# The out-projection of an attention kernel, made of three f16 products instead of one f32 product

## What is computed

```python
xn = layer_norm(layernorm(x), g1, b1); cn = layer_norm(context, g2, b2)
q, k, v = xn @ Wq.T, cn @ Wk.T, cn @ Wv.T              # 16 heads of 32
attn = softmax(q k^T / sqrt(32), masked)
x = x + (attn v) @ Wo.T + bo                           # the out-projection
x = x + quantised(layernorm(x)) @ quantised(W).T + bias  # blocks of 32, fp6 grid
```

## Time and profile before

| | |
|---|---|
| runs | 4388.42, 4397.13, 4397.69 us; median 4397.13 |
| span of the profiled execution | 4390.0 us (the page gives no other time of it) |
| busy: PE, DVE, POOL, ACT | 97%, 78%, 67%, 65% |
| f32 out-projection, 512 records | 228.7 us |
| mean granted TensorE clock | 0.998 |

### The profile page before, as it was taken

One profiled execution on the slowest core, in us unless ns is written; L12 is line 12 of the kernel. 1 busy time (PEld: TensorE's weight loads), 2 busy tenths in 40 slices (PEclk: granted clock), 3 DMA queues, 4 the chain that ended last, 5 costly groups with the idle time before them and its releaser, 6 DMA issues.

```text
span 4390.0 us, 89201 instructions
## 1 busy us (share of the span) xinstructions
PE 4263.7 (97%) x36496; PEld 1482.1 (34%) x36496; DVE 3402.3 (78%) x3967; ACT 2850.7 (65%) x5184; POOL 2936.2 (67%) x1830
## 2 busy tenths in 40 slices
PE   4999999999999999999999999999999999999999
PEld 2322343223432234322342223422234222342223
DVE  5789667886688865889658896689866898668985
ACT  3388844887448864588655886458854688546884
POOL 2199652996539964499534995359953699426993
PEclk9999999999999999999999999999999999999999
DMA  5266742657326573356733566335664366543664
GB/s 182 70 122 128 155 149 61 126 118 191 120 61 128 118 206 103 69 118 125 192 103 77 117 126 185 107 80 120 128 175 109 80 123 130 165 113 77 126 127 110
DMA packets 193708, 539.67 MB, mean 123 GB/s; under 512 B 28737, under 2 KB 102785, under 8 KB 152082
## 3 DMA queue, kind: packets, MB, share of 16 engines
q0 software_dynamic: 43776, 318.79, 36.3%
q1 hardware_dynamic: 149522, 215.17, 15.8%
HBM read 118.32 MB, written 21.01 MB: 32 GB/s over the span
## 4 chain that ended last, share of the span: by engine, by line
PE 70%; POOL 11%; DVE 7%; DMA 5%; issue 3%; ACT 2%; SPq 0%; POOLq 0%; DVEq 0%; ACTq 0%
PE banks L1116 18%; PE banks L1128 16%; PE banks L1024 16%; PE banks L1084 12%; DVE max_parts L664 5%; PE banks L1159 3%; POOL wkT_wvT_wqT L453 3%; DMA sums<-wkT_wvT_wqT 3%; PE banks L1018 3%; PE banks L993 2%; DMA wdT<-wkT_wvT_wqT 2%; POOL values L545 1%; ACT region L894 1%; POOL region L558 1%; POOL region L531 1%
## 5 line engine op out<-in xcount | busy, mean ns | idle before, releaser
L664 DVE TENSOR_REDUCE max_parts<-banks 128x2 f32<-128x1024 f32 x2048 | 2404.5, 1220 | 362.3 <-PE banks L1084 337.4
L894 ACT ACTIVATE region<-banks 128x512 f32<-128x512 f32 x4096 | 2190.0, 609 | 424.9 <-PE banks L1116 364.4
L453 POOL TENSOR_TENSOR wkT_wvT_wqT<-region 128x1024 f32<-128x1024 f32 x528 | 1348.7, 2752 | 447.0 <-PE banks L1128 327.5
L1116 PE MATMUL banks<-queries_stacked,keys_stacked 98*32 98x512 f16 x16384 | 1267.3, 382 | 12.7 <-ACT values L878 6.2
L1128 PE MATMUL banks<-region,values 128*32 128x512 f32 x8192 | 1075.6, 598 | 18.5 <-ACT region L894 14.8
L1116 PEld LDWEIGHTS banks<-queries_stacked,keys_stacked 98*32 98x32 f16 x16384 | 399.8, 95 | 1001.7 <-ACT region L894 625.5
L1084 PE MATMUL banks<-keys_stacked,queries_stacked 33*128 33x512 f16 x4096 | 716.9, 385 | 6.9 <-DVE max_parts L664 3.5
L1024 PE MATMUL banks<-region,wkT_wvT_wqT 128*128 128x512 f16 x2304 | 558.1, 381 | 12.8 <-DMA wkT_wvT_wqT<-weights_split 10.4
L1084 PEld LDWEIGHTS banks<-keys_stacked,queries_stacked 33*128 33x128 f16 x4096 | 183.4, 93 | 616.5 <-issue 376.5
L453 POOL TENSOR_TENSOR sums<-region 128x1024 f32<-128x1024 f32 x144 | 385.7, 2821 | 0.1
L433 POOL TENSOR_TENSOR region<-row_sums_inverse,region 128x512 f16<-128x512 f32 x80 | 93.3, 1166 | 430.4 <-ACT region L857 429.9
(11 more groups left out here) (99 smaller groups left out, 3247.8 us busy)
## 6 DMA issues: line engine op xcount, KB each, us to landing
wdT<-wkT_wvT_wqT POOLq DMA_DIRECT2D x96, 1024.0 KB, 12.2
wkT_wvT_wqT<-wkT_wvT_wqT POOLq DMA_DIRECT2D x80, 1024.0 KB, 7.6
sums<-wkT_wvT_wqT POOLq DMA_DIRECT2D x72, 1024.0 KB, 7.6
wkT_wvT_wqT<-sums POOLq DMA_DIRECT2D x40, 1024.0 KB, 7.5
region<-in_x SPq DMA_DIRECT2D x24, 1024.0 KB, 8.3
wkT_wvT_wqT<-weights_split SPq DMA_DIRECT2D x8, 3072.0 KB, 20.3
keys_stacked<-region SPq DMA_DIRECT2D x384, 64.0 KB, 2.0
keys_stacked<-sums SPq DMA_DIRECT2D x384, 64.0 KB, 2.0
```

The source lines that it names most:

```text
L453: e.tensor_tensor(SUMS[dst][:, half], PR[i][:, half], PR[i + 1][:, half], ALU.add).then_inc(s_pr, 1)
L664: e.tensor_reduce(mpart[:, buf, :, a, t, c], MXB[parity], AX.X, ALU.max).then_inc(s_mxd, 1)
L894: e.activation(PR[u % 4][:, j * HALF:j * HALF + HALF], score_bank(m % NU, kt, j)[0], ACT.Exp, scale=SCALE).then_inc(s_ex, 1)
L1116: mm = e.matmul(dst[HD * t:HD * t + HD, :], KA[0:STR, ds(ka + (j * C + (u + 1) * P + HD * t), HD)], QA[0:STR, ds(qa[j], HALF)], start=True ...
```

## The change

The out-projection goes through `contract_split`, with f16 high and low parts of both operands, twelve f16 matmuls a tile in place of four f32 ones. `WO` is loaded once at the start, scaled by 64 and split by ScalarE (high) and VectorE (low) into a free part of `QA`, stored to `wo_dram`, and loaded from there in each batch's last unit. The parts of a unit's outputs go into the second half of its `AO` space. For units 0 to 6 GpSimd makes them in the last unit, after its DMA issues: `parts(u)` is a copy to f16 and a subtraction. For unit 7 ScalarE makes the high and VectorE the low part. `x1_tile` scales by 1/64 as it adds.

```diff
@@
     split_dram = nc.dram_tensor("weights_split", [P, 3 * CC * D], F32, kind="Internal").ap()
     wd_dram = nc.dram_tensor("ffn_weights_quantised", [P, CC * D], F32, kind="Internal").ap()
+    wo_dram = nc.dram_tensor("out_weights_split", [P, CC * D], F32, kind="Internal").ap()
     levels = nc.dram_tensor("levels", [2, HALF], F16, kind="Internal").ap()
@@
         AO = QA[:, :].bitcast(F32)
         AO_UNIT = J * HALF // 2
+        ao_part = lambda n, part: QA[:, ds(n * 2 * AO_UNIT + AO_UNIT + part * HALF, HALF)]
+        WOS = WO[:, :, :].rearrange("p c d -> p (c d)")
+        WOP = split(WOS)
+        WO_FIRST = split(AO[:, 2 * AO_UNIT:4 * AO_UNIT])
         X1 = R[:, 0:4096].rearrange("p (i d) -> p i d", i=TT)
@@
             e.dma_start(affine[:, :, :], affine_in).then_inc(s_w, 16)
             tokens(1, x_chunks(0)[:, 1])
+            e.dma_start(WO[:, :, :], woT.rearrange("(c p) n -> p c n", p=P)).then_inc(s_wof, 16)
             e.wait_ge(s_wl, 3)
@@
             context_chunks = lambda b: ctx_in[ds(b, 1)].rearrange("a (c n p) d -> p (a c) n d", p=P, n=4)
+            e.wait_ge(s_wol, 1)
+            e.dma_start(wo_dram, AO[:, 2 * AO_UNIT:4 * AO_UNIT]).then_inc(s_wos, 16)
             e.wait_ge(s_wd, 16)
@@
                                 .broadcast_to([1, H // 2, C])).then_inc(s_mk, 16)
+                if b == 0:
+                    e.wait_ge(s_wos, 16)
                 for par in range(2):
@@
                         if 2 * g + q == NU - 1:
                             e.wait_ge(s_pv, (b * NU + NU - 2) * KT + 4 + 5)
-                            e.dma_start(WO[:, :, :], woT.rearrange("(c p) n -> p c n", p=P)).then_inc(s_wo, 16)
+                            e.dma_start(WOS, wo_dram).then_inc(s_wo, 16)
                         e.wait_ge(s_mc, b * NU + 2 * g + q + 1)
@@
+                        def parts(u):
+                            e.wait_ge(s_an, b * NU + u + 2)
+                            done = b * (NU - 1) + u
+                            ao = AO[:, ds(u * AO_UNIT, HALF)]
+                            e.tensor_copy(ao_part(u, 0), ao).then_inc(s_ah, 1)
+                            e.wait_ge(s_ah, done + 1)
+                            e.tensor_tensor(ao_part(u, 1), ao, ao_part(u, 0), ALU.subtract).then_inc(s_al, 1)
                         if end:
                             merge_last()
+                            parts(0)
                             merge(0, 1, one)
+                            parts(1)
+                            parts(2)
                             merge(1, 2, two)
+                            parts(3)
+                            parts(4)
                             merge(2, 3, three)
+                            parts(5)
+                            parts(6)
                             continue
@@
             for n in range(4):
                 fp6(XB[0][:, n, :]).then_inc(s_xd, 1)
+            e.wait_ge(s_wof, 16)
+            e.wait_ge(s_woh, 1)
+            e.scalar_tensor_tensor(WO_FIRST[:, 1, :, :].rearrange("p c d -> p (c d)"), WOS, W_SCALE,
+                                   WO_FIRST[:, 0, :, :].rearrange("p c d -> p (c d)"),
+                                   ALU.mult, ALU.subtract).then_inc(s_wol, 1)
@@
                         invert_rest()
                         normalise(m, n)
+                        e.wait_ge(s_an, m + 2)
+                        e.wait_ge(s_lh, b + 1)
+                        e.tensor_tensor(ao_part(n, 1), AO[:, ds(n * AO_UNIT, HALF)], ao_part(n, 0),
+                                        ALU.subtract).then_inc(s_ll, 1)
@@
                     e.wait_ge(s_op, b * TT + i + 1)
                     e.wait_ge(s_xb, b * TT + i + 1)
-                    e.tensor_tensor(X1[:, i, :], out_bank(i), X1[:, i, :], ALU.add).then_inc(s_x1, 1)
+                    e.scalar_tensor_tensor(X1[:, i, :], out_bank(i), 1.0 / W_SCALE, X1[:, i, :],
+                                           ALU.mult, ALU.add).then_inc(s_x1, 1)
                     e.wait_ge(s_x1, b * TT + i + 1)
@@
                 e.activation(WD[:, :, n * P:n * P + P], PS[:, n % 2, :].rearrange("p (c t) -> p c t", c=CC),
                              ACT.Copy).then_inc(s_tc, 1)
+            e.wait_ge(s_wof, 16)
+            e.wait_ge(s_cst, 2)
+            e.activation(WO_FIRST[:, 0, :, :].rearrange("p c d -> p (c d)"), WOS, ACT.Copy,
+                         scale=W_SCALE).then_inc(s_woh, 1)
             e.wait_ge(s_mdr, 32)
@@
                         outputs()
                         row_sums(m, KT)
+                        e.wait_ge(s_an, m + 2)
+                        e.activation(ao_part(n, 0), AO[:, ds(n * AO_UNIT, HALF)], ACT.Copy).then_inc(s_lh, 1)
@@
                     if i == 0:
                         e.wait_ge(s_wo, b * 16 + 16)
-                    if i % 4 == 0:
-                        e.wait_ge(s_an, b * NU + NU + i // 4)
+                    if i == 0:
+                        e.wait_ge(s_al, (b + 1) * (NU - 1))
+                    if i == 4:
+                        e.wait_ge(s_ll, b + 1)
                     if i == 2:
...
                     if i >= LEAD:
                         e.wait_ge(s_x1, b * TT + i - LEAD + 1)
-                    contract(out_bank(i), lambda cc: AO[:, ds((2 * cc + i // 4) * AO_UNIT + i % 4 * P, P)],
-                             lambda cc: WO[:, cc, :]).then_inc(s_op, 1)
+                    contract_split(out_bank(i), lambda s, cc: ao_part(2 * cc + i // 4, s)[:, ds(i % 4 * P, P)],
+                                   lambda s, cc: WOP[:, s, cc, :], iter(()), iter(())).then_inc(s_op, 1)
```

More of the change, by code:

```diff
@@ L240, in build @@
         s_wo = sem("out_projection_weights_loaded")
+        s_wof = sem("full_out_weights_loaded")
+        s_woh = sem("out_weights_high_part")
+        s_wol = sem("out_weights_low_part")
+        s_wos = sem("out_weights_stored")
+        s_ah = sem("outputs_high_part")
+        s_al = sem("outputs_low_part")
+        s_lh = sem("last_outputs_high_part")
+        s_ll = sem("last_outputs_low_part")
         s_po = sem("last_units_outputs_done")
```

## The result

The changed kernel takes 4409.33 us (median of 11 runs, 4406.38 to 4416.16) against 4396.29 for the one before (11 runs on the same chip, 4388.42 to 4407.73): ratio 1.0029, with a 95% interval of 1.0021 to 1.0038. It is slower by 13 us, where 25 were forecast. The profiled spans differ by 14.6 us.

The account below looks back on a forecast made before the run. TensorE, busy 97% of a 4390.0 us span, was taken as the bound. Out-projection delay 35.1, less gain 13.2, plus start 3.3, made +25.2 us on the runs' median of 4397.1: 4422 us, range 4400 to 4444.

Parts of the forecast that it names:

- Gain: 7 x 1.6 + 2.0 = 13.2 us: From the first out-projection matmul on, f16 products save 1.6 us in seven batches, 2.0 in the last; bounds 8.8 and 17.
- The ring: VectorE, GpSimd and ScalarE pass each out-projection tile round; everything behind tile 6's quantisation comes 2.1 us earlier a batch.
- nothing lost: Upper bound of the gain behind the first out-projection matmul: 17 us, if unit 7's low part delays nothing.
- T0's delay: The first out-projection matmul starts 35.1 us later over eight batches, as GpSimd's parts hold VectorE's additions; bounds 29 and 45.
- The price of the cast: GpSimd's copy of one part to f16 in the last unit: 0.95 us, bounds 0.69 and 1.26.
- The exclusion: VectorE's two-input additions and GpSimd's SBUF-reading work take turns by whole instructions; a part delays VectorE by 1.56 us.
- The slip of the first `merge`: Part 0 makes GpSimd's second DMA issue in the last unit slip about 1.7 us, absorbed by the queue: cost 0.
- rival (b): The first merge's slip in the last unit isn't absorbed: 1.7 us more in each of eight batches, 4436 us; chance 0.08.
- The start: Program start: the 1 MB store ahead of the projection weights costs 3.3 us, bounds 0 and 5; the weights' split costs 0.
- (a): GpSimd gets in only behind pairs of VectorE's additions, and its last subtraction ends last: +15.6 us, 4413; chance 0.15.
- (c): GpSimd and VectorE don't exclude each other in the last unit, parts stay hidden: -13.5 us, 4384; chance 0.13.
- (d): Partial exclusion: VectorE's additions end some 2 us late a batch, out-projection 1.2 us late, about no change; chance 0.09.

Follow-up runs that it names:

- parts-only run: Kernel before plus GpSimd's seven parts in the last unit and the first out-projection tile's wait for them, products still f32: 4426.47 us, ratio 1.0056.
- filler run: Kernel before plus two needless f32 matmuls in TensorE's pause ahead of tile 6's transposition: 4389.44 us, ratio 0.9966.
- its repetition: The changed kernel measured again, unaltered, against the kernel before: 4408.34 us, ratio 1.0016.
- last version: Changed kernel, GpSimd's casts of units 0-5 before its DMA issues, subtractions behind VectorE's first two pairs, unit 6 on VectorE, store behind loads: 4372.99 us, ratio 0.9934.
- memset run: Kernel before plus, for each of GpSimd's parts, three memsets instead of a cast and a subtraction, same waits, products f32: 4397.29 us, ratio 0.9996.
- run without parts: Changed kernel without GpSimd's seven parts, f16 matmuls taking blocks of the split weights instead of the outputs' parts: 4375.81 us against 4400.77, ratio 0.9939.
- the two versions with the train behind the first `merge`: Changed kernel, GpSimd only casting, six behind the first merge, VectorE subtracting: 4389.74 us; the same with the weights' store behind the first loads: 4389.35 us.

## Why the prediction was right in sign and wrong in size

**The step that failed** is the term "Gain: 7 x 1.6 + 2.0 = 13.2 us". Measured are 24.5 us from T0 to F. Of it:

- The ring's own part is 16.7 us. The changed kernel has 493.0 in sum. Before, a batch without a low clock at the pause takes 63.47 us from T0 to F (three batches of before, five of the parts-only run, six of the filler run) and the last one 65.46 (by the filler run): 7 x 63.47 + 65.46 = 509.7, and 509.7 - 493.0 = 16.7. That lies at my upper bound of 17 ("nothing lost"): tile 6 is quantised at T0 + 44.1 us in the mean, 2.1 earlier than the 46.16 of seven batches of before. I had let the front of the ring lose 0.5 us a batch to unit 7's low part; in the first batch `x1_tile(0)` starts at T0 + 6.03 (556.26 - 550.23), 1.5 later than before, and yet the end isn't later. No run tries where that time is made up; by the stages, none of it reaches the end.
- The other 7.9 us (517.6 - 509.7) are a low clock of before: 6.4 of it behind the pause in four batches, 1.5 in the seventh, where the clock fell at T0 itself and tile 6 was quantised at 47.67. I wrote "granted clock of 1.00" from the mean, 0.998, and expected of the new gaps only a fall that "would add to any case". I never looked at the windows just behind the 2.06 us pause that I had on the table. The filler run settles the 6.4: with the pause filled they are gone from T0 to F, and the ratio is 0.9966.

**The changed kernel's own low stretches** (mean clock 0.993) lie at two places. Those at T0 + 13, where TensorE waits for the ring, cost next to nothing: over the first seven batches of the changed kernel, its repetition and the last version, T0 to F is 61.7 us in the mean of the nine batches with one and 61.5 in the twelve without. Those ahead of T0 do cost. They are in all eight batches, twice as long in four of them, and there TensorE and not VectorE ends last. In the fourth batch VectorE's last addition ends at 2173.74, and TensorE comes to the row sum that needs it (2174.97) without a pause, because its groups of eight have just taken 1.9 us instead of 1.04:

```profile
2168.87 1.93 PE L1179 MATMUL banks<-region,values 128*32 128x512 f32 x8 [1.65 <-ACT region L943]
...
2170.85 1.94 PE L1210 MATMUL banks<-region,ones 128*32 128x512 f32 x8
2172.55 1.73 PE L1179 MATMUL banks<-region,values 128*32 128x512 f32 x8
2174.11 1.03 PE L1210 MATMUL banks<-region,ones 128*32 128x512 f32 x8
2174.97 1.03 PE L1210 MATMUL banks<-wkT_wvT_wqT,ones 128*32 128x512 f32 x8
2175.83 1.03 PE L1210 MATMUL banks<-sums,ones 128*32 128x512 f32 x8
```

T0 comes 3.05 us behind the last addition there, and 1.91 in the first two batches, where TensorE waits for that addition. Over the eight batches the distances sum to 19.4 us, 4.1 more than 8 x 1.91: an estimate of what the low clock ahead of T0 costs. It belongs to the next term.

**T0's delay: 36.2 measured, 35.1 forecast.** The sum is right and the terms are not. The last addition ends 38.7 us later in sum (forecast 8 x 5.2 = 41.6), of which the eight additions themselves are 22.2, the normalisation in front of them 8.0, and what comes earlier 8.5. I had put 4 us on the normalisation, nothing on anything earlier, and three parts on the additions. In truth part 4 had ended at 535.7, before the first addition at 536.2, and only parts 5 and 6 met them: 2.78 us for the two, 1.39 each where I took 1.56. What was earlier was the fifth pair, 3.10 us instead of 2.36 in the first batch, held by part 3. And I subtracted 6.5 us of slack behind the last addition where 2.5 were used up; the other 4 are the low clock ahead of T0, which I had priced at nothing. The errors cancel: that the sum comes out within 1.1 us is luck.

**The price of the cast.** I took 0.95 us by the earlier trace rows and named 0.69 as the lower bound. It is 0.60 alone. The Trainium skill's 769 ns ("GPSIMD Engine Reference", Performance versus the Vector engine) was nearer than my 0.95, and still too long for a conversion of 512 elements. The subtraction is 1.17, as taken.

**The exclusion.** Right, and shown from both sides: additions of 1.37 us in the median and up to 2.18 beside casts and subtractions, 1.22 in all 64 beside memsets, 9.54 for the eight once GpSimd's parts are elsewhere. That reading SBUF makes the difference rests on these two kinds of work; no other instruction that only writes was tried. My 1.9 to 2.3 us for each addition was wrong: only those that met parts 5 and 6 were held, at 1.82 in the median.

**The slip of the first `merge`.** Forecast 1.7, absorbed. Over eight batches its issue moves from U + 9.42 to U + 10.66 us, by 1.24, and the next one, behind a wait for it, only from 20.86 to 21.20. Absorbed but for 0.3 us; rival (b) is out.

**The start.** Forecast 3.3; the first projection comes 2.5 us later and the first U 3.1. With the store moved it comes at 65.73. Right. The split cost nothing, as taken (VectorE's next work, on the tokens, starts at 43.72 instead of 43.64); its part took 2.29 us and not 3.41.

**The other rivals.** (a), turns by twos, is out: in all eight batches GpSimd's last subtraction ends 3.0 us or more ahead of T0 and before VectorE's last addition, and TensorE goes from the row sums into the out-projection without a gap. Its number, 4413, is nearest to the result all the same, by accident; the mechanism it names isn't in the trace. (c), no exclusion, is out by the memset run and the parts-only run. (d) put the end of the additions at 2 us late; it was 4.8.

**Where TensorE pauses.** I named tiles 0, 4 and 5. Tile 0 (2.78 us in the first batch) and tile 5 (1.76) are there, tile 4 in four of the eight batches, and tile 6 keeps 1.04, which I had not named.

**What stays open.** In the run without parts and in the last version U to T0 is still 4 to 6 us longer in sum than before, mostly in the first two batches, where TensorE waits for the third accumulating DMA. Why that DMA lands later there wasn't tried. The filler run, which is the kernel before in that stage, shows the same wait in its first batch, and the same code moved by 3.7 us between two runs above, so part of it may be no more than that.

## What to carry to other kernels

Moving work onto an engine that looks idle is free only if it doesn't share something with the engine that sets the next deadline. Here 7 casts and 7 subtractions of GpSimd, 12 us of its time a batch, delayed VectorE's last addition by 4.8 us and T0 by 4.5. With six casts left on GpSimd, ahead of the additions, and the rest of that work on VectorE where it waits anyway, T0 came 0.5 late (302.4 against 298.5 in sum), and the change became a gain of 0.7%. And before a pause is priced, read the clock in narrow windows just behind it: a mean of 0.998 held some 8 us on the path, and a shorter matmul or a filler in the pause gave most of them back.

## What the runs showed of the hardware

- **A train of GpSimd casts can hold VectorE through several of them.** Single GpSimd instructions with a wait between them and VectorE's additions changed places one by one (0.9 and 2.0 us for a cast and a subtraction of 0.60 and 1.17). Casts in a row with no open wait between them held a VectorE instruction with two SBUF inputs for 2.0 to 3.2 us in the two versions with the train behind the first `merge`, every time to the train's end. In the last version they held it for 1.5 to 2.6 us, and in seven of the eight batches it got a turn behind the third or fourth cast, before the next. In the earlier trace rows it got one between two queued additions. What decides when the turn comes was not tried.
- **A memset of GpSimd takes nothing from VectorE's additions**: 168 memsets, 0.525 us in the median, and 64 additions between 1.216 and 1.227.
- **What a low clock costs depends on where it falls.** Four stretches of 3.4 us at 1.2 GHz behind TensorE's pauses of about 2 us cost the kernel before 6.4 us of its profiled span. The changed kernel has more than twice as much time at that level (mean clock 0.993 against 0.998). Its four stretches at T0 + 13 cost next to nothing, since TensorE waits there; those ahead of T0 cost some 4 us in sum, where they are long enough to make TensorE later than VectorE.
- **VectorE casts f32 to f16, 128x512, in 0.42 us**, GpSimd in 0.60. VectorE's scaled subtraction of 128x2048 with f16 output took 2.29 us, where the same form took 3.41 in the earlier trace rows at another moment of the start.
